# One-core model of mixtures, attention and scan: gated mixtures in 14 full tiles, folded values in relative attention

## What is computed

```python
# gated mixture: 8 experts with 176 inner rows, two of them per token, and a shared expert with 352
scores = softmax(x @ gate_w.T);  w = scores * in_top2
g, u = split(einsum('nh,eih->nei', x, experts_gate_up))
out = einsum('neh,ne->nh', einsum('nei,ehi->neh', silu(g) * u, experts_down), w)
shared = (silu(x @ shared_gate_w.T) * (x @ shared_up_w.T)) @ shared_down_w.T
out = out + sigmoid(x @ shared_expert_gate_w.T) * shared

# relative attention, 8 heads of 128
Q, K, V = heads(q @ w_qs) * scale, heads(q @ w_ks), heads(q @ w_vs)
a = softmax((Q + rel_embed_bias) @ K.T + relative_shift((Q + rel_pos_bias) @ rel_k.T))
out = merge_heads(a @ V) @ w_out + b_out
```

## Time and profile before

| | us |
|---|---|
| three executions | 2534.11, 2539.0, 2543.6 |
| their median | 2539.0 |
| the profiled execution | 2546.34 |
| its span, first to last instruction | 2544.6 |
| mean granted clock of TensorE in it | 0.871 |

### The profile page before, as it was taken

The page is one execution under the profiler, slowest core; times in us unless marked ns, Lnnn a source line. Parts: engine busy times, 40 slices in busy tenths (PEclk is TensorE's granted clock), DMA queues, the critical chain, the costliest instruction groups (busy, mean ns, idle before and its releaser), DMA issues. The chain is left out here.

```text
span 2544.6 us, 40452 instructions
## 1 busy us (share of the span) xinstructions
PE 2095.9 (82%) x13860; PEld 1658.8 (65%) x13860; DVE 1466.6 (58%) x3930; ACT 1004.4 (39%) x2247; POOL 131.7 (5%) x191
## 2 busy tenths in 40 slices
PE   3588777669977884999799899999899986778875
PEld 2455454469963223999799868888699973555543
DVE  6655454756668997666422337777633238555537
ACT  1345444332223321222444445555444435233444
POOL 1100000200001001000000000000000000000000
PEclk9779787869989995999799999999999988566668
DMA  5000000000000000000000024343200000000000
GB/s 149 14 1 1 1 1 1 29 1 1 0 1 0 0 0 33 1 0 0 1 1 0 19 87 126 122 126 122 79 1 0 0 1 0 1 1 0 0 1 16
DMA packets 47126, 59.75 MB, mean 23 GB/s; under 512 B 7089, under 2 KB 44689, under 8 KB 46323
## 3 DMA queue, kind: packets, MB, share of 16 engines
q1 hardware_dynamic: 47023, 58.43, 7.5%
HBM read 32.20 MB, written 26.21 MB: 23 GB/s over the span
## 5 line engine op out<-in xcount | busy, mean ns | idle before, releaser
L701 ACT ACTIVATE m2a_hid<-psum,m_b 128x256 f32<-128x256 f32 x256 | 100.5, 475 | 114.4 <-PE psum L55 114.3
L701 ACT ACTIVATE m2b_hid<-psum,m_b 128x256 f32<-128x256 f32 x256 | 100.4, 475 | 113.5 <-PE psum L55 113.4
L686 PE MATMUL psum<-m_w,m2a_hid 128*128 128x128 f32 x1024 | 126.2, 277 | 0.0
L686 PE MATMUL psum<-m_w,m2b_hid 128*128 128x128 f32 x1024 | 125.5, 276 | 0.0
L719 DVE SCALAR_TENSOR_TENSOR m2b_acc<-psum,m2b_gates,m2b_acc 128x128 f32<-128x128 f32 x128 | 39.0, 347 | 147.6 <-PE psum L686 147.6
L719 DVE SCALAR_TENSOR_TENSOR m2a_acc<-psum,m2a_gates,m2a_acc 128x128 f32<-128x128 f32 x128 | 39.0, 347 | 147.3 <-PE psum L686 147.3
L686 PEld LDWEIGHTS psum<-m_w,m2a_hid 128*128 128x128 f32 x1024 | 122.1, 194 | 0.6
L686 PEld LDWEIGHTS psum<-m_w,m2b_hid 128*128 128x128 f32 x1024 | 121.5, 193 | 0.6
L2079 ACT ACTIVATE a_p<-a_p,a_nmax 128x256 f32<-128x256 f32 x128 | 63.9, 500 | 141.5 <-DVE a_nmax L2106 141.5
L1822 DVE TENSOR_REDUCE a_nmax<-psum 128x2 f32<-128x512 f32 x128 | 82.8, 687 | 50.1 <-PE psum L1663 50.1
L1056 DVE TENSOR_TENSOR_SCAN a1s_clamped<-a1s_clamp_coef,a1s_bounds 128x1024 f32<-128x1024 f32 x48 | 108.7, 2266 | 0.0
(11 more groups left out here) (608 smaller groups left out, 5624.2 us busy)
## 6 DMA issues: line engine op xcount, KB each, us to landing
a_scratch<-a_pos SPq DMA_DIRECT2D x64, 384.0 KB, 2.7
a_shifted<-a_scratch SPq DMA_DIRECT2D x64, 256.0 KB, 3.1
m_w<-in_m_w SPq DMA_DIRECT2D x1, 2048.0 KB
arena<-in_m_w SPq DMA_DIRECT2D x1, 2048.0 KB, 8.9
arena<-in_m_up SPq DMA_DIRECT2D x1, 1760.0 KB, 7.2
a_w<-in_a_w SPq DMA_DIRECT2D x1, 1536.0 KB, 7.7
out<-X SPq DMA_DIRECT2D x1, 1024.0 KB, 5.1
m_down<-in_m_down SPq DMA_DIRECT2D x1, 880.0 KB
```

What stands on the lines that cost most here:

```text
L686: last = nc.tensor.matmul(ps_y(e % 2)[:, t * D:(t + 1) * D], hid[:, e % 2, c * SEQ + t * P:c * SEQ + (t + 1) * P], m.m2_w2[:, e, c, :], st ...
L701: last = nc.scalar.activation(hid[:, e % 2, c * SEQ:(c + 1) * SEQ], ps_up(e % 2)[:, c * SEQ:(c + 1) * SEQ], ACT.Gelu, bias=m.m2_b1[:, e * ...
```

## The change

**Gated mixture.** The inner rows of all experts stand one behind the other, 8 x 176 + 352 = 1760, padded to 1792 = 14 tiles of 128. A step takes two tiles, so there are seven to a batch, with three fp32r products for each of two gate tiles and two up tiles. Since a tile can hold rows of two experts, the gate is applied to the hidden rows: the gates are split into two parts (`parts`, 18 columns), turned to 18 rows (`parts_T`, sixteen transposes at the start), and two fp32r products per step with a table of zeros and ones (`pick`) spread them to the rows of the two tiles (`ps_share`). DVE multiplies silu by the spread gates and then by the up half. The down products of all seven steps add up in one PSUM bank, and DVE adds that to `X` once a batch. Down products follow two steps behind the up-step.

**Relative attention.** In the first block the value weights of each head are turned and multiplied by that head's part of `w_out`, and the product takes the place of the value weights. In the main block the output products (L2067), the copy `oT` on ACT and the add per head on DVE are gone; the values are made with the turned probabilities as weights, four products of 128 columns, and the heads add up in PSUM.

The diff, cut to what runs on the engines (`...` marks what is left out):

```diff
@@ moe_gated @@
+    S, OWNERS = 7, 18
...
+            def spread(n, k, p):
+                for t in range(2):
+                    last = nc.tensor.matmul(ps_share(k % 2)[:, t * SEQ:(t + 1) * SEQ], pick[:, (2 * p + t) * P:(2 * p + t + 1) * P],
+                                            parts_T[:, bass.ds(n * SEQ, SEQ)], start=True, stop=True)
+                last.then_inc(share_ready, 1)
+
+            def up(n, q, k):
+                pe.wait_ge(hid_ready, q - 1)
+                products(n, k, k % S, ps_gate, 0).then_inc(gate_ready, 1)
+                spread(n, k, k % S)
+                products(n, k, k % S, ps_up, 1).then_inc(up_ready, 1)
+
+            def down(q, k, n_before):
+                p, u = k % S, k // S % 2
+                pe.wait_ge(hid_ready, q + 1)
+                if p == 0 and n_before is not None:
+                    pe.wait_ge(y_used, n_before)
+                for t in range(PAIR):
+                    for c in range(2):
+                        last = nc.tensor.matmul(ps_y(u)[:, t * D:(t + 1) * D], hid[:, p % 4, c * SEQ + t * P:c * SEQ + (t + 1) * P],
+                                                m.m1_down[:, 2 * p + c, :], start=(p == 0 and t == 0 and c == 0),
+                                                stop=(p == S - 1 and c == 1), skip_group_check=True)
+                if p == S - 1:
+                    last.then_inc(y_ready, 1)
...
+            for k in range(2):
+                products(0, k, k, ps_gate, 0).then_inc(gate_ready, 1)
+                products(0, k, k, ps_up, 1).then_inc(up_ready, 1)
+            pe.wait_ge(parts_ready, 1)
+            for g in range(4):
+                for t in range(4):
+                    last = nc.tensor.transpose(m.psum[0:OWNERS, TURN_BANK[g], t * P:(t + 1) * P],
+                                               parts[:, 4 * g + t, :].bitcast(F32), m.ident[:, :])
+                last.then_inc(turned, 1)
+            pe.wait_ge(pick_ready, 1)
+            pe.wait_ge(even_moved, 1)
+            spread(0, 0, 0)
+            pe.wait_ge(odd_moved, 1)
+            spread(0, 1, 1)
+            pe.wait_ge(even_moved, 2)
+            pe.wait_ge(odd_moved, 2)
+            for k in range(2, 2 * S):
+                up(k // S, k, k)
+                down(k - 2, k - 2, None)
+            with pe.Fori(1, NB // 2) as i:
...
+                    up(2 * i + k // S, 2 * S * i + k, k)
+                    down(2 * S * i + k - 2, (k - 2) % (2 * S), 2 * i + k // S - 1)
...
+            def residual(n, u):
+                dve.wait_ge(y_ready, n + 1)
+                nc.vector.scalar_tensor_tensor(out=pair_of(m.X, n), in0=ps_y(u), scalar=0.5, in1=pair_of(m.X, n),
+                                               op0=ALU.mult, op1=ALU.add).then_inc(y_used, 1)
+                nc.vector.drain()
+                norm_begin(nc, xn, lambda t: tile_of(m.X, n, t))
...
+            def step(q, k):
+                b = k % 2
+                dve.wait_ge(silu_ready, q + 1)
+                dve.wait_ge(share_ready, q + 1)
+                nc.vector.tensor_tensor(silu[:, b, :], silu[:, b, :], ps_share(b), ALU.mult)
+                nc.vector.drain()
+                dve.wait_ge(up_ready, q + 1)
+                nc.vector.tensor_tensor(hid[:, k % S % 4, :], silu[:, b, :], ps_up(b), ALU.mult).then_inc(hid_ready, 1)
             routing.vector(dve)
-            expert_steps(dve, S, step)
+            nc.vector.tensor_copy(parts[:, :, 0:9], m.gates[:, :, :])
+            nc.vector.drain()
+            nc.vector.tensor_tensor(parts[:, :, 9:18], m.gates[:, :, :], parts[:, :, 0:9].bitcast(F32), ALU.subtract).then_inc(parts_ready, 1)
...
+                    if k % S == 1:
+                        residual(2 * i + k // S - 1, (k // S + 1) % 2)
...
@@ relative_attention @@
+            pe.wait_ge(m.loaded["a2"], m.total["a2"])
+            pe.wait_ge(xT_moved, 2)
+            for h in range(H):
+                last = nc.tensor.transpose(m.psum[:, h // 4, h % 4 * P:(h % 4 + 1) * P], m.a2_w[:, 2, h * P:(h + 1) * P], m.ident[:, :])
+            last.then_inc(vT_ready, 1)
...
+                if h == 4:
+                    pe.wait_ge(vT_moved, 1)
+                    pe.wait_ge(xT_moved, 4)
+                    for k in range(H):
+                        last = nc.tensor.matmul(m.psum[:, 2 + k // 4, k % 4 * P:(k % 4 + 1) * P], v_turned[:, k * P:(k + 1) * P], m.a2_out[:, k, :],
+                                                start=True, stop=True)
...
-                pe.wait_ge(o_moved, H * n + h + 1)
-                for kt in range(2):
-                    last = nc.tensor.matmul(ps_o, v[:, h, kt, :], pT[:, kt, :], start=(kt == 0), stop=(kt == 1))
...
-            def share(u, n, h):
...
-                    last = nc.tensor.matmul(ps_y[:, t * D:(t + 1) * D], oT[:, h % 2, t * P:(t + 1) * P], m.a2_out[:, h, :], start=True, stop=True)
+                if h == 0:
+                    pe.wait_ge(y_used, n + 1)
+                for t in range(PAIR):
+                    for kt in range(2):
+                        last = nc.tensor.matmul(ps_y[:, t, :], pT[:, kt, t * P:(t + 1) * P], v[:, h, kt, :],
+                                                start=(h == 0 and kt == 0), stop=(h == H - 1 and kt == 1))
...
-            def values(u, n, h):
...
-                nc.scalar.activation(oT[:, h % 2, :], ps_o, ACT.Copy).then_inc(o_moved, 1)
...
-            def share(u, n, h):
-                nc.vector.drain()
...
-                before = m.a2_b_out[:, :] if h == 0 else acc[:, :]
-                nc.vector.tensor_tensor(acc[:, :], ps_y, before, ALU.add).then_inc(y_used, 1)
+            def result(u, n, h):
                 if h == H - 1:
+                    nc.vector.drain()
+                    dve.wait_ge(y_ready, H * n + H)
+                    nc.vector.tensor_tensor(acc[:, :].rearrange("p (t f) -> p t f", t=PAIR), ps_y,
+                                            m.a2_b_out[:, :].rearrange("p (t f) -> p t f", t=PAIR), ALU.add).then_inc(y_used, 1)
```

More of the change, by code:

```diff
@@ L558, in _ @@
         def _(pe):
[L559 to L572, removed]
-                for t in range(PAIR):
[L574 to L577, removed]
@@ L578, in _, with products @@
-            routing.tensor(pe)
-            up(0, 0)
-            expert_steps(pe, S, step)
+            def products(n, k, p, dst, half):
+                for t in range(2):
+                    last = split_matmul(nc, dst(k % 2)[:, t * SEQ:(t + 1) * SEQ],
+                                        [w[:, 2 * p + t, half * P:(half + 1) * P] for w in m.m1_up], split_tokens_T(m, n))
+                return last
+            def spread(n, k, p):
+                for t in range(2):
+                    last = nc.tensor.matmul(ps_share(k % 2)[:, t * SEQ:(t + 1) * SEQ], pick[:, (2 * p + t) * P:(2 * p + t + 1) * P],
+                                            parts_T[:, bass.ds(n * SEQ, SEQ)], start=True, stop=True)
+                last.then_inc(share_ready, 1)
@@ L582, in _ @@
+            for k in range(2 * S - 2, 2 * S):
+                down((NB // 2 - 1) * 2 * S + k, k, None)
         @block.scalar
@@ L585, in _ @@
             nc.scalar.preload_act_table(ACT.Silu)
[L587 to L590, removed]
+            def step(q, k):
+                act.wait_ge(gate_ready, q + 1)
+                nc.scalar.activation(silu[:, k % 2, :], ps_gate(k % 2), ACT.Silu).then_inc(silu_ready, 1)
+            for k in range(2 * S):
+                step(k, k)
+                if k == 1:
+                    for g in (0, 2):
+                        act.wait_ge(turned, g + 1)
+                        nc.scalar.activation(parts_T[:, g * 512:(g + 1) * 512], m.psum[0:OWNERS, TURN_BANK[g], :],
+                                             ACT.Copy).then_inc(even_moved, 1)
@@ L592, in _ @@
+            with act.Fori(1, NB // 2) as i:
+                for k in range(2 * S):
+                    step(2 * S * i + k, k)
         @block.vector
         def _(dve):
[L594 to L607, removed]
-                    nc.vector.drain()
-                    residual_begin(nc, m, xn, n, acc[:, :], 0.5)
-                    if last_step:
-                        residual_end(nc, dve, m, xn, n)
@@ L631, in _ @@
+            with dve.Fori(1, NB // 2) as i:
+                for k in range(2 * S):
+                    step(2 * S * i + k, k)
+                    if k % S == 1:
+                        residual(2 * i + k // S - 1, (k // S + 1) % 2)
+                    if k % S == 3:
+                        residual_end(nc, dve, m, xn, 2 * i + k // S - 1)
+            residual(NB - 1, 1)
+            residual_end(nc, dve, m, xn, NB - 1)
         @block.gpsimd
         def _(pool):
+            pool.wait_ge(pick_loaded, 16)
@@ L2142, in _ @@
                 dve.sem_inc(pos_written[j], 16)
-            run(dve, [(0, maxima), (-1, transposes), (0, division), (4, projections), (-3, end), (-2, share)])
```

(1 more changed line is left out.)

109 lines of the change are left out of this document (57 added, 52 removed).

## The result

The median fell from 2536.6 us (four runs; the three known at the forecast had 2539.0) to 2475.1 (four runs, 2472.1 to 2477.1): ratio 0.9752, 95% interval 0.9727 to 0.9777. The profiled execution took 2477.06 us, span 2475.2. The changed kernel is clearly faster, by 61 us where 104 was forecast, and the time lies above the range.

What follows compares the result with a forecast made beforehand. What PE streams was taken to bound both changed stages. Two gated calls won 84 us, splitting weights cost 0.5, attention won 21: 104.5 off the median of 2539.0, so 2434 us, range 2424 to 2452.

Steps and rivals of the forecast that it cites:

- The spreading products: Gated step: two products of 18 rows and 256 columns, priced at 0.117 us each like neighbouring split products; step 2.54 us.
- upper bound of 2 x 0.43: Gated step: the most the two 18-row products could cost, 0.43 us each, at the f32 pace.
- rival (d): Gated steps fall to seven, but 18-row products run at the f32 pace: 70 us less gain, 2504; chance 0.04.
- Weight loads of 128 columns: Gated split products: loads take 189 ns against 155 with 88 columns, but stay off the path; 0.117 us a product.
- rival (b): Gated split products: 128-column weight loads come onto the path, 34 ns each; 46 us less gain, 2480; chance 0.04.
- PE's input in time: Gated steps: DVE ends hidden rows at about 3.0 us, PE needs them at 5.08; 2.1 us spare.
- The start: Gated stage: PE's stream resumes at 561.0, 6 us later; half of 3.2 us lost to clock; 42 won per call.
- Attention step: Attention loop: a step falls from 5.21 to 4.80 us if PE still sets it; 26.2 us over 64 steps.
- Ends of batches: Attention: DVE's lateness paid a second time at ACT, 0.5 us more each, seven times 3.5; ends about 39.6 apart.
- ACT's margin "gone": Attention step: ACT's keys, 0.5 us early before, would keep only about 0.05 to 0.1 us ahead of PE's load.
- Fold: Attention preparation: eight transposes free in PE's 4.02 us wait, eight products cost 1.8 us, or nothing if the clock rises earlier.
- The 21: Attention's total gain in us: 26.2 from the steps, less 3.5 at ends of batches, less 1.8 for folding.

## Why the prediction was wrong, and where it was right

- **The spreading products: the failed step.** "I take 0.117, since 88 and 128 rows cost the same." The product's own price was right: 0.12. What the sum lacked, and put at nothing, was the change between 18 and 128 rows, 0.37 us a step, 41 of the 44.5 us in 112 steps. The 88 rows stand on the cheap side, with 96 and 128, so they were no witness for 18. With 128 rows the step was 2.57 against the 2.54 forecast. Two products and the change together take 0.60 us, inside the prediction's own upper bound of 2 x 0.43; but only rival (d) used that bound, by another mechanism (2504), and the range left it out. A nearer witness stood in the trace of the kernel before, in an attention stage with products of 32 rows (L1269):

```profile
208.81 0.39 PE L1276 MATMUL psum<-global_hidden,global_ident 128*128 128x256 bf16 x2
209.14 0.39 PE L1269 MATMUL psum<-global_qT,global_kT 32*128 32x256 f32 x2
...
209.51 0.39 PE L1276 MATMUL psum<-global_hidden,global_ident 128*128 128x256 bf16 x2
209.74 0.38 PE L1299 MATMUL psum<-ident,global_ov 128*128 128x128 f32 x2
```

  The same two products of 128 rows take 0.33 us to the next product where that has 32 rows, and 0.23 where it has 128; most of the 18 and 30 such places of that trace show the same. The 0.1 more is what the changed kernel has ahead of its first spreading product (0.21 against 0.12). The price of the way back cannot be read from these rows.
- **Weight loads of 128 columns** off the path: right, the run with 128 rows shows 0.12 us a product. That the time lies near rival (b)'s 2480 is chance. The loads' own length was read too kindly: 189 against 155 ns is 1.22 to 1, not in proportion to the columns (1.45 to 1); only the difference, 34 ns, is that of the estimate of 107 against 73.
- **PE's input in time**: right, no wait of PE between 560 and 705 us.
- **The start**: right. PE's stream resumed at 559.12 (561.0 forecast, in a stage that began 1.4 earlier), and one set of down products ran at the lower clock (1.74 us in the rows below, 1.05 later). Before the change the clock had been low ahead of the wait of 3.9 us too, which the prediction does not say: it was 0.50 from 536 to 550, with PE busy all that time.

```profile
559.12 0.35 PE L53 MATMUL psum<-m1a_XT_high,m_raw_high 128*128 128x256 f32 x1 [1.56 <-DVE m1a_hid L660]
...
562.08 1.74 PE L592 MATMUL psum<-m_down,m1a_hid 128*128 128x128 f32 x8
```

- **Attention step** 4.80: right. The sum as written, 5.21 - 0.45 - 0.04, would be 4.72; the new values cost 0.04 more, so the sign is a slip, and 4.80 is what was carried on.
- **Ends of batches**: 40.05 apart, not 39.6. The prediction's mechanism exists (it shows once the bank is free, at 39.47) but lay behind a wait that it had not seen: nowhere does it ask when DVE reads the result's new PSUM area.
- **ACT's margin "gone"**: wrong, read at the weight load instead of at the products. It did no harm to the sum of the steps.
- **Fold**: 1.8 us of cost forecast; the preparation became 2.1 shorter (from the first transposes to the first projections 25.72 before, 23.63 after). Two things are in this. The position products start 1.3 us earlier after the stage's first transposes (6.38 against 7.66); this is not shown to be the fold's, since it is 6.48 in the run with the gated half alone, which folds nothing (last two rows below). And with the weight transposes in the wait of the earlier trace rows they find the clock up: the granted clock is 0.89 from 1416 to 1420 and 1.00 in the next four us, where before it was 0.50 from 1464 to 1468 and 0.82 in the next four. That is the case in which the prediction let the fold cost nothing. From the first position product to the first projections it is 18.06 and 18.11 us in the two traces without the fold and 17.25 with it, its eight products included: the fold itself wins 0.8. The changed kernel, then the gated half alone:

```profile
1415.33 1.79 PE L2006 MATMUL psum<-ident,a_w 128*128 128x128 f32 x8
1418.27 7.13 PE L2020 MATMUL psum<-a2r_positions,a2r_w_rel 96*128 96x512 f32 x16 [1.15 <-DMA a2r_positions<-in_a_positions]
1425.24 1.95 PE L2014 MATMUL psum<-a_out,a2r_v_turned 128*128 128x128 f32 x16
```
```profile
1418.11 3.65 PE L1998 MATMUL psum<-ident,XN 128*128 128x128 f32 x16 [4.34 <-PEq L78]
1424.59 16.64 PE L2006 MATMUL psum<-a2r_positions,a2r_w_rel 96*128 96x512 f32 x32 [2.83 <-DMA a2r_positions<-in_a_positions]
```

  So 26.2 - 7.1 (seven ends at 1.0 more) + 2.1 = 21.2. The 21 came out by luck: the ends cost 3.6 us more than forecast, the preparation 3.9 less, and 1.3 of these are not the fold's.

## What to carry to other kernels

When an operand with few rows is put between full products, price the change of rows on either side, not the product alone, and look in the trace at hand for products of few rows between full ones. Padding with zeros to the neighbours' count took 38 us off the median here (2475.1 to 2436.6). A PE that is busy all the time may still be losing; count its records per stretch, or PEld's busy time, before and after. When a sum moves into PSUM for a whole batch, ask who reads it at the end, and whether the next batch can begin elsewhere.

## What was not expected of the hardware

Among products of 128 rows, those of 96 and 128 rows start 0.12 us apart, and fp32 products of 88 rows cost what those of 128 do (0.81 us for four). Products of 18 and 64 rows cost 0.37 us more for each way there and back, shown as busy time. In the run with one more ACT instruction a weight load waited 0.46 us for its operand, and the products behind it began 0.23 later behind the scores (1.09 against 0.86).
